# Layer 3's score vectors from natural rows, and the norms of layers 1 to 3 scaled by ACT

## What is computed

```python
x = _layernorm(x + L0(x, adj))   # batch norms around two dense layers
x = _layernorm(x + L1(x, adj))   # edge attention, 4 heads, softmax over edges
x = _layernorm(x + L2(x, adj))   # three dense layers, each mixed by adj*adj, relu
x = _layernorm(x + L3(x, adj))   # dense graph attention

def L3(h, adj, W, a):
    Wh = h @ W
    s1, s2 = Wh @ a[:F], Wh @ a[F:]
    e = leaky_relu(s1[:, :, None] + s2[:, None, :], 0.2)
    e = where(adj == 0, -inf, e)
    return softmax(e) @ Wh
```

## Time and profile before

| what | value |
|---|---|
| median of 3 runs | 656.43 us (655.6 to 658.11) |
| the profiled execution, whole | 657.9 us |
| its span, first to last instruction | 655.8 us |
| busy: PE, DVE, ACT, POOL | 88%, 72%, 47%, 34% of the span |
| mean granted clock of TensorE | 0.935 of 2.4 GHz |
| step to step in the middle of the kernel | 48.7 us |

### The profile page before, as it was taken

How to read it: one execution, slowest core, us unless ns; L and a number is a source line. 1 busy time by engine, 2 the same in 40 slices (tenths; PEclk the granted TensorE clock), 3 DMA queues, 4 the chain that set the end, 5 groups by cost and what they waited for, 6 DMA issues and landing times.

```text
span 655.8 us, 11248 instructions
## 1 busy us (share of the span) xinstructions
PE 576.3 (88%) x3666; PEld 503.4 (77%) x3666; DVE 472.6 (72%) x1366; ACT 306.2 (47%) x557; POOL 223.1 (34%) x238
## 2 busy tenths in 40 slices
PE   2999797799977639999999899999999999899763
PEld 2888444588855629898999899899899899799653
DVE  5588586898753383448669869869869869766885
ACT  1576774355522303334563463563563553642660
POOL 6830700665434250404404504404404305213220
PEclk9999798799977768999999999999999999999777
DMA  6322000221000000000000100100100100100002
GB/s 173 95 74 86 1 0 18 78 66 41 23 1 0 1 0 1 1 1 1 1 1 0 33 0 0 32 0 0 32 0 0 32 0 0 32 1 22 13 0 64
DMA packets 28380, 15.24 MB, mean 23 GB/s; under 512 B 2320, under 2 KB 28048, under 8 KB 28352
## 3 DMA queue, kind: packets, MB, share of 16 engines
q1 hardware_dynamic: 27792, 13.65, 7.5%
q0 software_dynamic: 560, 1.25, 0.5%
HBM read 10.69 MB, written 4.19 MB: 23 GB/s over the span
## 4 chain that ended last, share of the span: by engine, by line
PE 45%; DVE 20%; issue 9%; ACT 4%; POOL 3%; DVEq 1%; POOLq 0%; ACTq 0%
PE psum L221 7%; PE psum L223 7%; PE psum L222 7%; PE psum L1312 5%; DVE ob L215 4%; PE psum L1445 4%; DVE ln_st L180 3%; DVE keep_x L215 3%; PE psum L1333 3%; PE psum L1319 2%; PE psum L1397 2%; PE psum L1323 2%; ACT soft L1135 2%; PE psum L1387 2%; POOL ln_r L197 2%
## 5 line engine op out<-in xcount | busy, mean ns | idle before, releaser
L197 POOL TENSOR_TENSOR ln_r<-ln_v,mhalf 128x8 f32<-128x8 f32 x32 | 55.4, 1730 | 298.6 <-DVE ln_v L191 298.6
L215 DVE TENSOR_SCALAR keep_x<-keep_x,ln_ag,ln_r 128x128 f32<-128x128 f32 (+1 forms) x192 | 78.3, 483 | 4.9 <-POOL ln_r L197 4.8
L1116 ACT ACTIVATE h<-psum 128x512 f32<-128x512 f32 x64 | 38.2, 598 | 49.7 <-PE psum L223 49.7
L1445 PE MATMUL psum<-l2w_s,h 128*128 128x128 f32 x512 | 59.6, 275 | 0.0
L1445 PEld LDWEIGHTS psum<-l2w_s,h 128*128 128x128 f32 x512 | 59.0, 192 | 0.7
L221 PE MATMUL psum<-qt_hi,l2w_s_hi 128*128 128x512 f32 x128 | 52.5, 410 | 0.0
L223 PE MATMUL psum<-qt_hi,l2w_s_lo 128*128 128x512 f32 x128 | 50.5, 394 | 0.0
L222 PE MATMUL psum<-qt_lo,l2w_s_hi 128*128 128x512 f32 x128 | 50.4, 394 | 0.0
L816 DVE SCALAR_TENSOR_TENSOR h_lo<-psum,h_hi 128x1024 fp32r<-128x1024 f32 x16 | 19.6, 1225 | 35.8 <-ACT h_hi L1107 35.8
L1135 ACT ACTIVATE soft<-soft,s1c 128x256 f32<-128x256 f32 x64 | 26.8, 498 | 29.9 <-DVE m L838 29.8
L180 DVE BATCH_NORM_STATS2 ln_st<-keep_x 128x6 f32<-128x128 f32 (+1 forms) x192 | 39.2, 277 | 1.4 <-DVE keep_x L215 0.9
(11 more groups left out here) (225 smaller groups left out, 1778.2 us busy)
## 6 DMA issues: line engine op xcount, KB each, us to landing
xin<-in_x SPq DMA_DIRECT2D x64, 128.0 KB, 2.3
out_x<-ob SPq DMA_DIRECT2D x32, 128.0 KB, 1.9
l2w_raw<-in_l2w POOLq DMA_DIRECT2D x1, 512.0 KB, 6.8
adjs<-in_adj SPq DMA_DIRECT2D x1, 256.0 KB, 2.7
adjs<-in_adj_t SPq DMA_DIRECT2D x1, 256.0 KB, 3.0
l2w_s<-in_l2w POOLq DMA_DIRECT2D x1, 256.0 KB, 6.6
w_raw<-in_w_t SPq DMA_DIRECT2D x1, 128.0 KB, 3.3
w2t<-in_w_t SPq DMA_DIRECT2D x1, 128.0 KB, 3.2
```

The costliest lines, as they stand in the source:

```text
L197: pool.tensor_tensor(ln.r[:].rearrange("p s k -> p (s k)"), ln.v[:].rearrange("p s k -> p (s k)"), mhalf[:], ALU.pow).then_inc(ln.rstd, 1)
L215: i = dve.tensor_scalar(dst_of(k // 2, k % 2), y(s, k // 2, k % 2), ln.ag[:, s, k, 0:1], ln.r[:, s, k:k + 1], ALU.subtract, ALU.mult)
L1116: act.activation(h2[:, s, g, :], bank(4 + g)[:, 0, :], ACT.Relu).then_inc(h2_out, 1)
L1445: i = pe.matmul(bank(s)[:, 0, k * D:(k + 1) * D], h2[:, s, g, j * N + t * P:j * N + (t + 1) * P], l2w3_s[:, g, :], start=(g == 0), stop=(g ...
```

## The change

The score vectors of layer 3 are computed from the rows as they lie. The weights that they need (`wa`) are now spread over all partitions, two vectors of 128. `own_scores` on DVE multiplies each 128x128 block with each vector and sums along the row, 16 instructions for a group, into `s12`. PE then spreads the second score by transposing a broadcast column (`spread3`), which leaves it in every partition. `take_x3`, `turn3`, `turned3` and PE's `scores3` are gone, with the buffers `x3`, `xt3`, `wa2_bc` and `s1c`.

For the norms of layers 1 to 3 within the steps, ACT computes `r * x + b` in place (`ln_scale`), with `b = -mean * r`. DVE negates the mean (in `ln_var_eps`), and POOL multiplies it by `r` behind the power (in `ln_power`). Both functions serve layer 0 too, whose norms DVE still applies, as it does the very first of layer 1 and the last ones behind the loop.

The order moves as well: on DVE the statistics of layer 2 (`variance(p - 1, ln2)`) go from behind `weighted_low` to behind `pt_low`, and on POOL the power of layer 2 goes ahead of `weigh`.

```diff
@@ ln_var_eps, ln_power @@
             dve.wait_ge(ln.mean, p + 1)
+            dve.tensor_scalar(ln.m[:].rearrange("p s k -> p (s k)"), ln.ag[:].rearrange("p s k c -> p (s k) c")[:, :, 0],
+                              -1.0, None, ALU.mult)
...
-                               ALU.pow).then_inc(ln.rstd, 1)
+                               ALU.pow).then_inc(ln.root, 1)
+            pool.wait_ge(ln.root, p + 1)
+            pool.tensor_tensor(ln.b[:].rearrange("p s k -> p (s k)"), ln.m[:].rearrange("p s k -> p (s k)"),
+                               ln.r[:].rearrange("p s k -> p (s k)"), ALU.mult).then_inc(ln.rstd, 1)
+        def ln_scale(act, y, p, s, ln):
+
+            act.wait_ge(ln.rstd, p + 1)
+            for k in range(4):
+                i = act.activation(y(s, k // 2, k % 2), y(s, k // 2, k % 2), ACT.Identity, bias=ln.b[:, s, k:k + 1],
+                                   scale=ln.r[:, s, k:k + 1])
+            i.then_inc(ln.done, 1)
@@ POOL, step @@
+                if behind:
+                    ln_power(pool, p - 1, ln2)
                 if two_ahead:
                     for s in range(2):
                         weigh(s, 2 * (p + 2) + s, False)
-                if behind:
-                    ln_power(pool, p - 1, ln2)
                 if ahead:
                     ln_power(pool, p + 1, ln1)
-                if behind:
-                    take_x3(p - 1, not two_behind)
@@ DVE @@
+            def own_scores(p):
+
+                for s in range(2):
+                    q = 2 * p + s
+
+                    wait_apart(dve, dc, ln2.done, q + 1)
+                    for c in range(2):
+                        for k in range(4):
+                            i = dve.scalar_tensor_tensor(out=soft[:, s, k, c * D:(c + 1) * D], in0=xn[:, q, k // 2, k % 2, :], scalar=1.0, in1=wa[:, c, :],
+                                                         op0=ALU.mult, op1=ALU.mult, accum_out=s12[:, s, c, k:k + 1])
+                    i.then_inc(s12_ok, 1)
@@ DVE, step @@
                 for s in range(2):
                     pt_low(p, s)
+                if behind:
+                    variance(p - 1, ln2, not two_behind)
...
-                if behind:
-                    variance(p - 1, ln2, not two_behind)
...
                 if behind:
-                    apply(p - 1, ln2)
-                if ahead:
-                    apply(p + 1, ln1)
+                    own_scores(p - 1)
...
-                s3_low(p, 0)
-                if two_behind:
-                    norm3(p - 2)
-                s3_low(p, 1)
+                for s in range(2):
+                    s3_low(p, s)
@@ ACT, step @@
                 for s in range(2):
                     qt_high(p, s)
+                    if behind:
+                        ln_scale(act, row(p - 1), p - 1, s, ln2)
...
                 for g in range(2, GB):
                     h2_relu(p, 1, g)
+                    if ahead and g == 2:
+                        ln_scale(act, row(p + 1), p + 1, 0, ln1)
                 s3_high(p, 0)
-                if behind:
-                    turned3(p - 1)
+                if ahead:
+                    ln_scale(act, row(p + 1), p + 1, 1, ln1)
                 s3_high(p, 1)
+                if two_behind:
+                    for s in range(2):
+                        ln_scale(act, last_sum, p - 2, s, ln3)
                 if behind:
                     sum_scores(p - 1)
@@ PE @@
-            pe.matmul(bank(7)[:, 0, 4:6], l3wt_s[:], l3a_s[:], start=True, stop=True)
+            for k in range(2):
+                pe.matmul(bank(7)[:, 0, (k + 1) * D:(k + 2) * D], l3a_s[:, k:k + 1].broadcast_to([P, P]), l3wt_s[:], start=True, stop=True)
...
+            def spread3(p, s):
+
+                pe.wait_ge(s12_ok, 2 * p + s + 1)
                 for j in range(2):
                     for t in range(T):
+                        c = j * N + t * P
+                        i = pe.transpose(bank(4 + s)[:, 0, c:c + P], s12[:, s, 1, 2 * t + j:2 * t + j + 1].broadcast_to([P, P]), ident[:])
+                i.then_inc(s2_done, 1)
...
                     for s in range(2):
-                        turn3(p - 1, s)
+                        spread3(p - 1, s)
...
-                if behind:
-                    for s in range(2):
-                        scores3(p - 1, s)
```

More of the change, by code:

```diff
@@ L96, in build @@
         l2w1_s = hilo("l2w1_s", [P, H2A])
-        l2w2_raw, xt3 = in_turn(lambda c: sb("l2w2_raw", [P, GA, H2B], scope=c), lambda c: sb("xt3", [P, 2, W], scope=c))
+        l2w2_raw = sb("l2w2_raw", [P, GA, H2B])
         l2w2_s = hilo("l2w2_s", [P, GA, H2B])
@@ L102, in build @@
         l3a_s = sb("l3a_s", [P, 2])
-        wa = sb("wa", [P, 2])
-        wa2_bc = sb("wa2_bc", [P, P])
+        wa = sb("wa", [P, 2, D])
         bnp = sb("bnp", [P, 9])
@@ L128, in build @@
         picked, a_edge_done, log_ready = sem("picked"), sem("a_edge_done"), sem("log_ready")
-        weights_split, wgt_ready, wa2_ready = sem("weights_split"), sem("wgt_ready"), sem("wa2_ready")
+        weights_split, wgt_ready = sem("weights_split"), sem("wgt_ready")
         bst1 = sb("bst1", [P, H0 // P, Q, 6])
@@ L170, in __init__ @@
                 self.r = sb(f"ln{tag}_r", [P, 2, 4])
+                self.m = sb(f"ln{tag}_m", [P, 2, 4])
+                self.b = sb(f"ln{tag}_b", [P, 2, 4])
+                self.root = sem(f"ln{tag}_root")
         ln0, ln1, ln2, ln3 = (LayerNorm(k) for k in range(4))
@@ L242, in build @@
         o2_done = sem("o2_done")
-        x3_ready, t3_done, xt3_out = sem("x3_ready"), sem("t3_done"), sem("xt3_out")
-        s2_done, s1_out, tm_done, m_step = sem("s2_done"), sem("s1_out"), sem("tm_done"), sem("m_step")
+        s12_ok, s2_done, tm_done, m_step = sem("s12_ok"), sem("s2_done"), sem("tm_done"), sem("m_step")
         zt_ready, lk_ready, ex_ready = sem("zt_ready"), sem("lk_ready"), sem("ex_ready")
@@ L250, in build, with row, last_sum @@
         stored = [sem("stored0"), sem("stored1")]
+        def row(p):
+            return lambda s, t, j: xn[:, 2 * p + s, t, j, :]
+        def last_sum(s, t, j):
+            return ob[:, s, t, j, :]
         x_nat = x.rearrange("b (t n) d -> n t b d", n=P)
@@ L294, in build @@
         wv = sb("wv", [P, 2, ET, 2, D])
-        sc, x3 = in_turn(lambda c: sb("sc", [P, 4, E], scope=c), lambda c: sb("x3", [P, 2, T, 2, D], scope=c))
+        sc = sb("sc", [P, 4, E])
         ecol_i = sb("ecol_i", [P, 2, ET], I32)
@@ L305, in build @@
         m3 = sb("m3", [P, 2, 4])
-        s1c = sb("s1c", [P, 2, 4])
+        s12 = sb("s12", [P, 2, 2, 4])
         zm = sb("zm", [P, 3, 2, 4])
@@ L451, in _ @@
             pool.tensor_scalar(reset[:], same[:], 1.0, BIG, ALU.subtract, ALU.mult)
-            pool.tensor_scalar(wa2_bc[:], ones[:], wa[:, 1:2], None, ALU.mult).then_inc(wa2_ready, 1)
             pool.wait_ge(adj_dst_out, 1)
@@ L501, in split_x, with split_x3 @@
                 pool.tensor_tensor(xs[1][:, s], xn[:, q], xs[0][:, s], ALU.subtract).then_inc(xs_lo, 1)
-            def take_x3(p, first):
+            def split_x3(p, first):
                 for s in range(2):
@@ L510, in take_x3 @@
                     if not first:
-                        pool.wait_ge(t3_done, q - 1)
-                    pool.tensor_copy(x3[:, s], xn[:, q]).then_inc(x3_ready, 1)
-            def split_x3(p, first):
-                for s in range(2):
-                    q = 2 * p + s
-                    if not first:
-                        wait_apart(pool, pz, ax_done, q - 1)
+                        pool.wait_ge(ax_done, q - 1)
                     pool.tensor_copy(x3_hi[:, s], xn[:, q]).then_inc(x3_hi_ok, 1)
@@ L566, in _ @@
             ln_power(pool, IT - 1, ln2)
-            take_x3(IT - 1, False)
             split_x3(IT - 1, False)
@@ L691, in _ @@
                          bnp[:, 6:7], bnp[:, 7:8], bnp[:, 8:9], 2).then_inc(bn2_ready, 1)
-            def row(p):
-                return lambda s, t, j: xn[:, 2 * p + s, t, j, :]
             def variance(p, ln, first):
@@ L828, in s3_low @@
                                   s3[0][:, s], ALU.subtract).then_inc(s3_lo, 1)
+            def own_scores(p):
[7 more added lines that the diff above has]
+                    i.then_inc(s12_ok, 1)
             def scores3(p):
                 for s in range(2):
-                    q = 2 * p + s
-                    dve.wait_ge(s2_done, q + 1)
-                    dve.tensor_copy(s1c[:, s, :], bank(6 + s)[:, 0, 0:4]).then_inc(s1_out, 1)
+                    wait_apart(dve, dc, s2_done, 2 * p + s + 1)
                     for k in range(4):
@@ L843, in scores3 @@
                 dve.wait_ge(tm_done, 2 * p + 2)
-                dve.wait_ge(s1_out, 2 * p + 2)
-                dve.tensor_tensor(zm[:, 0], m3[:], s1c[:], ALU.add).then_inc(m_step, 1)
+                dve.wait_ge(s12_ok, 2 * p + 2)
+                dve.tensor_tensor(zm[:, 0], m3[:], s12[:, :, 0, :], ALU.add).then_inc(m_step, 1)
                 dve.wait_ge(m_step, 3 * p + 1)
```

(21 more changed lines are left out.)

## The result

The kernel after takes 661.22 us in the median (659.83 to 664.54), the one before 656.43 in the same rounds: ratio 1.0072, 95% interval 1.0039 to 1.0105. It is slower, as forecast, but by 4.8 us where the forecast had 11.

A forecast was written before the change was run, and what follows sets the result against it. PE was taken to bound the kernel, 88% busy. Setup +0.9, first boundary with scores +1.4, four loop boundaries +4.8, last step +2.5 and tail +1.4 made 11.0 on 656.4: 667 us, range 655 to 674.

The forecast's parts named there:

- The boundary: Stretch from `narrow(p, 1)` to the next `hidden1`: claimed 1.6 us gained, while PE's idle grows from 1.59 to 3.35 us.
- E to H: From the first PE instruction behind `narrow(p, 1)` to the start of the next `hidden1`: 11.86 us before, forecast 10.25.
- The clock falls at each of the six boundaries: PE's longer idle ahead of `hidden1` in steps 2 to 7 halves its clock nearly everywhere: 667 us, chance 0.60.
- it holds below about 2.0 us: Rival: PE's clock stays up if its idle ahead of `hidden1` is below about 2.0 us; 651 us, chance 0.17.
- The size of a fall: PE's low clock behind a wait lasts 6.8 us, 0.6 of it in the idle, and costs 2.8 us.
- the four loop boundaries: Ends of loop steps ahead of `hidden1`: each 1.6 us gained and 2.8 lost to the clock, together +4.8 us.
- the boundary into step 2: First boundary with scores, no layer-3 norms yet: 0.6 us gained, 2.0 lost to a clock fall at 7 in 10, +1.4.
- The last step: Boundary into the last step, without `attend1`: 10.5 us becomes 10.25, PE's gap grows to 4.2, +2.5 us.
- The tail: Behind the last step: `own_scores` makes the reduction 2.0 us late, about half comes back, 0.45 for the last norm; +1.4.
- The setup: First layer-0 and first layer-1 norm lie bare, 0.45 us each for negation and product: +0.9.
- the case of half the falls: Rival: PE's clock falls at every second boundary only, half of 13 us, so 660 us; chance 0.10.
- the likeliest case: Clock falls nearly everywhere: 661 to 673 us, for scalings of 0.28 to 0.50 and slow stretches of 5 to 6.8 us.

The follow-up runs named there:

- e3: Kernel before with only the norms of layers 1 to 3 moved to ACT, scores left as they were on PE: 654.37 us, ratio 0.9951.
- e1: Kernel after plus ten unread matmuls per step (fourteen in the last) on PE ahead of the first `hidden1`: 651.96 us, ratio 0.991 to the kernel before.
- e5: Kernel before plus three unread DVE reductions ahead of `pt_low`, so `hidden1` starts 1.7 us later: 676.85 us, ratio 1.0312.
- e6: Kernel after with half of ACT's layer 3 scalings moved ahead of the second `s3_high`, no added matmuls: 655.9 us, ratio 0.9981 to the kernel before.
- e2: Kernel after plus four unread matmuls per step on PE ahead of the first `hidden1`: 655.19 us, ratio 0.9971 to the kernel before.
- e4: Kernel after with the norms back on DVE, so only the scores differ from the kernel before: 679.36 us, ratio 1.0322.

## Why the prediction was right, and where it was wrong

- **The boundary: right.** E to H was forecast as 10.25 us and is 10.36 (1.6 gained, measured 1.5), and 9.5 into step 2, measured 9.53. PE's waits were forecast as 2.6, four times 3.35, and 4.2; they are 2.36, 3.20 to 3.25, and 4.26. The prices behind it held: scalings 0.38 (0.39), own sums 0.25 (0.215), POOL's product 0.35 (0.28). The own sums that ran beside POOL's power (447.03 to 448.67) were no slower for it, 0.21 to 0.24 us from start to start. e3 shows that the norms make this gain in the steps 3 to 7.
- **The clock falls at each of the six boundaries: right.** e1 and e5 show it from both sides, by taking the idle away from the changed kernel and by bringing it into the old one. The rival "it holds below about 2.0 us" agrees with waits of 1.45 and 1.59; its condition was not met. Its sum was 651 us, and e1, in which the clock does hold, took 651.96, so the rest of the sum came out about right.
- **The size of a fall: the step that failed.** "A fall lasts 6.8 us, of which I let 0.6 lie in the idle itself: 6.2 x 0.45 = 2.8 us". Four of the six lasted 3.4 us and cost 1.3 to 1.5. In step 4 the fall did last 6.8 and cost 2.6, as priced. Both falls that I priced by the earlier trace rows were of the long kind, and no low stretch in the trace of before is shorter than 6.8 us, so nothing there showed that 3.4 is possible; I took two cases for the rule (my lower bound of 5 us came from no row). The spans differ by 2.2 us where the sum said 11.0. Of these 8.8 us the four loop boundaries make 4.0 (+4.8 forecast, +0.8 measured) and the boundary into step 2 another 0.6; the points below hold the rest.
- **The last step: over-sized.** +2.5 forecast, +1.1 measured. The fall there is a long one, but costs 1.3. It begins 1.29 us before `hidden1`, where I had let 0.6 lie in the idle. And before the change PE waits once more inside this step, 4 us behind `hidden1`, which I had not counted:

```profile
572.56 0.39 PE L221 MATMUL psum<-wgt_hi,h_hi 128*128 128x256 f32 x1 [0.96 <-DVE h_lo L816]
```

After the change PE has no such wait (busy for all of the 36.70 us from `hidden1` to E): the slower matmuls fill it, and 0.96 us of the fall cost nothing.

- **The tail: half of it seen, the sum not decided.** `own_scores` does delay the reduction: it starts 21.3 us behind the last step's E (627.55 less 606.24), and started 19.95 behind it before. That is 1.4 late where I said 2.0. But the end is 51.9 us behind that E before and 51.7 after: in this pair all of the delay came back, and the 0.45 of the last norm with it, where I let half come back. Which wait took it up was not tested. With the same instructions behind the last step, e1 takes 53.0 us from that E to the end and e6 50.7, so one pair can't decide 1.4 us.
- **The setup: not decided.** +0.9 forecast, -0.4 in this pair. The first `hidden1` starts anywhere from 246.3 to 249.9 us in profiles of kernels whose instructions up to there differ little, so one pair can't show 0.9 us. Such scatter may also be why the spans give 2.2 us and the medians 4.8; which stretch holds the remaining 2.6 is open.
- **A slip in a rival.** The falls in my sum add up to 16.0 us (2.0 and five times 2.8), not 13: the case of half the falls is 8 less than 667, 659 and not 660. The forecast does not rest on it.

That 661 lies within my 655 to 674 is partly luck. I had widened that range for falls that fail to come; they all came, and most were half as long. It also touches the lower edge of the likeliest case (661), but that edge stood for cheaper scalings and falls of 5 us, and neither was measured.

## What to carry to other kernels

In this kernel, work taken from the busiest engine was worth only what ended sooner at its next wait; the rest became idle, and a wait of 2.3 us or more ahead of a burst of matmuls mostly cost the clock, and with it another 1.3 to 2.6 us. So shorten the path of the late engines first (the norms alone: 654.4 us), and when matmuls are removed from the shadow of a wait, see whether the wait is now long enough to bring the clock down. If it is, matmuls that nobody reads can recover it: the kernel after went from 662 to 652 us with ten per step, and to 648 once the scalings had moved too.

## What the runs showed of the hardware that was not expected

- TensorE's low stretches in the steps came in two lengths, 3.4 and 6.8 us, and the length went with how long PE still waited after their start: 0.86 to 1.29 us in each of the long ones at a `hidden1` (four in the two profiles of the kernel after, one each in e2 and e5), and at most 0.57 us, or not at all, in all 21 short ones of these and of e6. Why is open: only the coincidence was seen.
- Behind waits of 2.27 to 2.38 us ahead of `hidden1` the clock mostly falls: five of five times in e6 (and behind the 3.35 at the last), into step 2 in both profiles of the kernel after, three of four in e2. Behind 1.86 us (into the last step of e4) and less it fell nowhere in the steps.
- A DVE multiply with its sum read out takes 0.215 us from start to start for 128 columns of f32 with both inputs in SBUF, less than the 0.40 of a norm of the same size.
- POOL's product of 128x8 takes 0.20 us beside 1.64 for the power of the same shape.
